# Bias terms rounded sooner, and the integers of the last tiles by another way, in an attention and int8 feed-forward kernel

## What is computed

```python
def layernorm(x): return (x - mean(x)) / sqrt(var(x) + 1e-5)

q      = layernorm(x)                                  # (8, 512, 512)
scores = einsum('bqd,bkd->bqk', q, ctx) / 0.72
attn   = softmax(scores) * mask
x1     = x + (einsum('bqk,bkd->bqd', attn, ctx) + attn_bias) @ W

h       = layernorm(x1)
x_scale = max(amax(abs(h), -1), 1e-6) / 127
x_q     = clip(round(h / x_scale), -128, 127)          # int8
out     = x1 + (x_q @ weight_q.T) * x_scale * weight_scale + ffn_bias
```

## Time and profile before

| | |
|---|---|
| time, median of 3 runs | 327.37 us (326.77 to 328.47) |
| profiled execution, time and span | 327.26 us, 325.1 us |
| TensorE matmul busy | 316.5 us, 97% |
| VectorE busy | 288.8 us, 89% |
| ScalarE, GpSimd busy | 236.0 us, 73%; 222.9 us, 69% |

### The profile page before, as it was taken

How to read it: one execution, slowest core, us unless ns; L and a number is a source line. 1 busy time by engine, 2 the same in 40 slices (tenths; PEclk the granted TensorE clock), 3 DMA queues, 4 the chain that set the end, 5 groups by cost and what they waited for, 6 DMA issues and landing times.

```text
span 325.1 us, 6047 instructions
## 1 busy us (share of the span) xinstructions
PE 316.5 (97%) x1522; PEld 254.8 (78%) x1522; DVE 288.8 (89%) x568; ACT 236.0 (73%) x440; POOL 222.9 (69%) x359
## 2 busy tenths in 40 slices
PE   7999999999999999999999999999999999999993
PEld 7878877778877777887777788877777887777781
DVE  2888889999999999999999999999999999989986
ACT  4466778787778778777777877787787777756651
POOL 3274667677787767678776777877677787766563
PEclk9999999999999999999999999999999999999999
DMA  7997848667485855658595664748667485432002
GB/s 214 272 226 187 196 147 205 190 158 202 146 210 163 219 171 159 196 145 210 161 213 174 161 197 150 203 161 209 178 155 199 144 211 162 126 116 98 33 33 97
DMA packets 69248, 55.26 MB, mean 170 GB/s; under 512 B 21488, under 2 KB 51952, under 8 KB 69232
## 3 DMA queue, kind: packets, MB, share of 16 engines
q1 hardware_dynamic: 61312, 40.65, 49.2%
q10 hardware_dynamic: 7920, 14.42, 13.2%
HBM read 34.87 MB, written 16.25 MB: 157 GB/s over the span
## 4 chain that ended last, share of the span: by engine, by line
PE 90%; DMA 3%; DVE 2%; ACT 1%; SPq 1%; issue 0%; ACTq 0%
PE ps_scores L555 9%; PE ps_scores L557 9%; PE ps_scores L556 9%; PE ps_attn L557 9%; PE ps_attn L555 9%; PE ps_attn L556 9%; PE ps_vw L555 8%; PE ps_vw L557 8%; PE ps_vw L556 8%; PE ps_ffn L716 8%; PE ps_pt L547 4%; DMA x_in<-in_x_dram 2%; DMA ctx_in<-in_ctx_dram 1%; SPq L426 1%; PE ps_pt L543 1%; PE ps_ut L547 1%
## 5 line engine op out<-in xcount | busy, mean ns | idle before, releaser
L1277 POOL TENSOR_TENSOR ct_lo<-ct_raw,ct_hi 128x512 fp32r<-128x512 f32 x28 | 36.2, 1293 | 20.9 <-ACT ct_hi L768 20.9
L555 PE MATMUL ps_vw<-w_hi,ct_hi 128*128 128x512 f32 x116 | 50.5, 435 | 0.0
L555 PE MATMUL ps_attn<-vw_hi,pt_hi 128*128 128x512 f32 x124 | 48.9, 395 | 0.0
L555 PE MATMUL ps_scores<-ct_hi,xt_hi 128*128 128x512 f32 x124 | 48.7, 393 | 0.0
L557 PE MATMUL ps_attn<-vw_hi,pt_lo 128*128 128x512 f32 x124 | 48.4, 391 | 0.0
L557 PE MATMUL ps_scores<-ct_hi,xt_lo 128*128 128x512 f32 x124 | 48.3, 389 | 0.0
L556 PE MATMUL ps_scores<-ct_lo,xt_hi 128*128 128x512 f32 x124 | 48.2, 389 | 0.0
L556 PE MATMUL ps_attn<-vw_lo,pt_hi 128*128 128x512 f32 x124 | 48.2, 389 | 0.0
L1270 POOL TENSOR_TENSOR out_tile<-ffn_out,x_plus 128x512 f32<-128x512 f32 x31 | 40.3, 1299 | 8.6 <-DVE ffn_out L1020 8.6
L557 PE MATMUL ps_vw<-w_hi,ct_lo 128*128 128x512 f32 x116 | 45.4, 391 | 0.0
L556 PE MATMUL ps_vw<-w_lo,ct_hi 128*128 128x512 f32 x116 | 45.3, 390 | 0.0
(11 more groups left out here) (163 smaller groups left out, 776.6 us busy)
## 6 DMA issues: line engine op xcount, KB each, us to landing
x_in<-in_x_dram SPq DMA_DIRECT2D x32, 256.0 KB, 3.1
mask_in<-in_mask_BxSxS_fk_dram SPq DMA_DIRECT2D x32, 256.0 KB, 3.2
norm_rows<-x_norm ACTq DMA_DIRECT2D x30, 256.0 KB, 2.3
x_blocks<-norm_rows SPq DMA_DIRECT2D x120, 64.0 KB, 2.4
ctx_in<-in_ctx_dram SPq DMA_DIRECT2D x56, 128.0 KB, 3.3
out_dram<-out_tile ACTq DMA_DIRECT2D x25, 256.0 KB, 2.5
out_dram<-out_tile SPq DMA_DIRECT2D x6, 256.0 KB, 2.0
ctx_in<-in_ctx_dram SPq DMA_DIRECT2D x4, 256.0 KB, 3.9
```

The lines of the kernel that those rows point to most:

```text
L555: nc.tensor.matmul(bank_, lhs_hi(t), rhs_hi(t), start=(t == 0), stop=False)
L1277: nc.gpsimd.tensor_tensor(ct_lo[:, batch_of(n), :, j * P:(j + 1) * P], ct_raw[:, slot(n, 2), :, :], ct_hi[:, batch_of(n), :, j * P:(j + 1) ...
```

## The change

Four parts. bias_terms is rounded by ScalarE ahead of the first step, and VectorE makes bias_terms_lo ahead of the first two vw_lo. BY_PE goes from 26 to 28, so the integers of tiles 26 and 27 are transposed by DMA, issued by SyncE in the last batch's steps 0 and 1; the product of tile 27 on TensorE and its scaling on VectorE move behind the attention of tile 29 and behind pt_lo of tile 30. The integers of tile 31 are rounded, transposed and copied in two halves, into two banks (ps_ut, ps_pt). The last outputs are made as a product with the weight scales and then a scale-and-add, in place of a product with both scales and then a sum. The diff below goes through SyncE, TensorE (turn_integers, feed_forward, the last steps), ScalarE (ahead of the first step, where the rounding stood behind two split_vw before; clear_integers; the last steps) and VectorE (round_last, finish_last, the first step, the last steps) in this order.

```diff
-BY_PE = TAIL - 2
+BY_PE = TAIL
...
+        last_ut_banks = [ps_ut, ps_pt]
...
-                if exists(base, d - 2) and not last_batch(base):
+                if exists(base, d - 2) and (in_loop(base) or base + d - 2 < BY_PE):
                     wait_count(sp, x1_int_ready, base, d - 2 + 1)
...
                     if is_tile(base, n, LAST):
-                        pe.wait_ge(last_x1_int_ready, 1)
-                    else:
-                        wait_count(pe, x1_int_ready, base, n + 1)
+                        pe.wait_ge(xq_t_ready, base + n - BY_PE)
+                        for h in range(2):
+                            pe.wait_ge(last_x1_int_ready, h + 1)
+                            for t in range(h * NT // 2, (h + 1) * NT // 2):
+                                turned = nc.tensor.transpose(last_ut_banks[h][:, :].bitcast(BF16)[:, t * P:(t + 1) * P],
+                                                             x1_int[:, slot(n, 2), t * P:(t + 1) * P],
+                                                             identity16[:, :])
+                            turned.then_inc(ut_done, 1)
+                        return
+                    wait_count(pe, x1_int_ready, base, n + 1)
...
                             for t in range(NT):
+                                if t == NT // 2:
+                                    pe.wait_ge(xq_t_ready, base + n + 2 - BY_PE)
...
-                    if d > 0 and exists(base, d):
+                    if d > 0 and exists(base, d) and not is_tile(base, d - 2, TAIL):
                         feed_forward(d - 3)
                     if exists(base, d - 1):
                         attend(d - 1)
+                    if is_tile(base, d - 2, TAIL):
+                        feed_forward(d - 3)
                     if exists(base, d + 1):
                         turn_probs(d)
+                    if is_tile(base, d - 2, BY_PE):
                         turn_integers(d - 2)
...
             normalise(HEAD, PER_BATCH + 1)
+            act.wait_ge(bias_terms_ready, NT)
+            nc.scalar.activation(bias_terms_hi[:, :], bias_terms[:, :], ACT.Copy).then_inc(bias_hi_ready, 1)
...
+                    if is_tile(base, n, LAST):
+                        for h in range(2):
+                            act.wait_ge(ut_done, base + n + 1 + h - BY_PE)
+                            nc.scalar.activation(flat(xq_t[:, slot(n, 2), h * NT // 2:(h + 1) * NT // 2, :]),
+                                                 last_ut_banks[h][:, :].bitcast(BF16)[:, half_of(h)],
+                                                 ACT.Copy).then_inc(xq_t_ready, 1)
+                        return
...
-                late = last_batch(base) and exists(base, d + 1)
+                late = is_tile(base, d - 2, BY_PE)
...
+                    for h in range(2):
+                        nc.vector.tensor_scalar(x1_round[:, slot(n, 2), half_of(h)], x1_neg[:, slot(n, 2), half_of(h)],
+                                                col(neg_gain, n), ROUND_MAGIC, ALU.mult,
+                                                ALU.add).then_inc(last_x1_round_ready, 1)
...
+                        nc.vector.tensor_scalar(x1_int[:, slot(n, 2), half_of(h)], x1_round[:, slot(n, 2), half_of(h)],
+                                                ROUND_MAGIC, None, ALU.subtract).then_inc(last_x1_int_ready, 1)
...
-                        nc.vector.scalar_tensor_tensor(out=last_out[:, half_of(h)], in0=last_ffn_banks[h][:, 0:HALF],
-                                                       scalar=col(x_scale, n), in1=wscale_wide[:, half_of(h)],
-                                                       op0=ALU.mult, op1=ALU.mult).then_inc(last_ffn_out_ready, 1)
+                        nc.vector.tensor_tensor(last_out[:, half_of(h)], last_ffn_banks[h][:, 0:HALF],
+                                                wscale_wide[:, half_of(h)], ALU.mult).then_inc(last_ffn_out_ready, 1)
                         dve.wait_ge(last_ffn_out_ready, h + 1)
-                        nc.vector.tensor_tensor(last_out[:, half_of(h)], last_out[:, half_of(h)],
-                                                last_x1_plus[:, half_of(h)], ALU.add).then_inc(last_out_ready, 1)
+                        nc.vector.scalar_tensor_tensor(out=last_out[:, half_of(h)], in0=last_out[:, half_of(h)],
+                                                       scalar=col(x_scale, n), in1=last_x1_plus[:, half_of(h)],
+                                                       op0=ALU.mult, op1=ALU.add).then_inc(last_out_ready, 1)
...
                 if is_tile(base, d, 0):
+                    dve.wait_ge(bias_hi_ready, 1)
+                    lo_part(bias_terms_lo[:, :], bias_terms[:, :], bias_terms_hi[:, :], bias_lo_ready)
                     for t in range(2):
                         split_vw(base, d + t, first_vw_banks[t])
-                    dve.wait_ge(bias_hi_ready, 1)
-                    lo_part(bias_terms_lo[:, :], bias_terms[:, :], bias_terms_hi[:, :], bias_lo_ready)
...
-                if last_batch(base) and d > 0 and exists(base, d):
+                if last_batch(base) and d > 0 and exists(base, d) and not is_tile(base, d - 2, TAIL):
                     scale_ffn(d - 3)
...
                 if exists(base, d) and not is_tile(base, d, LAST):
                     split_probs(d)
+                if is_tile(base, d - 2, TAIL):
+                    scale_ffn(d - 3)
```

More of the change, by code:

```diff
@@ L697, in feed_forward @@
                 def feed_forward(n):
-                    if last_batch(base):
+                    if isinstance(base, int) and base + n >= BY_PE:
                         pe.wait_ge(xq_t_ready, base + n + 1 - BY_PE)
@@ L879, in step @@
                         split_vw(base, d + t, first_vw_banks[t])
-                    act.wait_ge(bias_terms_ready, NT)
-                    nc.scalar.activation(bias_terms_hi[:, :], bias_terms[:, :], ACT.Copy).then_inc(bias_hi_ready, 1)
                     act.wait_ge(first_xt_done, 2)
@@ L1083, in round_last @@
                     dve.wait_ge(neg_gain_ready, TILES)
[L1084 to L1090, removed]
+                    for h in range(2):
+                        nc.vector.tensor_scalar(x1_round[:, slot(n, 2), half_of(h)], x1_neg[:, slot(n, 2), half_of(h)],
+                                                col(neg_gain, n), ROUND_MAGIC, ALU.mult,
+                                                ALU.add).then_inc(last_x1_round_ready, 1)
+                        dve.wait_ge(last_x1_round_ready, h + 1)
+                        dve.wait_ge(ut_done, TILES - 2 - BY_PE)
+                        nc.vector.tensor_scalar(x1_int[:, slot(n, 2), half_of(h)], x1_round[:, slot(n, 2), half_of(h)],
+                                                ROUND_MAGIC, None, ALU.subtract).then_inc(last_x1_int_ready, 1)
                 def finish_last():
```

## The result

The changed kernel took 332.23 us (median of 4 runs, 331.88 to 333.73) against 327.92 for the kernel before on the same chip: a ratio of the means of 1.0141, 95% interval 1.0093 to 1.019. The profiled execution took 332.10 us, its span is 330.3 us against 325.1. The direction was forecast; the size, 330.9 us with a range to 332.3, was not quite: the median is 1.3 us above the forecast, at the very edge of the range, and the mean of the four runs, 332.5, is outside it.

What follows compares the result with a forecast made beforehand. TensorE was taken as the bound, nine tenths of the chain. First step 0.2, stall 3.27 and end 0.2 made 3.66 us on 327.26: 330.9 us, range 329.3 to 332.3.

Steps and rivals of the forecast that it cites:

- the last one issued 1.32 later: SyncE's queue, last steps: the last of tile 31's four loads is issued 1.32 us after the first, 1.75 for four.
- D: Last steps: VectorE's turn of tile 31's rows, and all that follows it, late by 3.06 us; 2.6 to 4.1 by landing.
- a rival at 0.06: TensorE's clock falls to 1.2 GHz in the new gap; scores of tile 31 take 2.84 us more: 333.7 us, chance 0.06.
- the first step: VectorE's early subtraction loses the shared port to GpSimd, so TensorE's bias product starts later: +0.2 us.
- The bound, and SyncE's queue: TensorE bounds; in SyncE's in-order queue, the wait for tile 27's integers holds up output 25's store and tile 31's loads.
- the prediction's other case: First step: VectorE takes the port first and the bias product starts 0.6 us sooner: 330.1 us in all, chance 0.28.
- GpSimd ahead: First step: of two nearly tied starts, 21.17 and 21.24, GpSimd's comes first and holds the shared port.
- GpSimd's queue: Last steps: rstd of tile 29 waits behind the sum of output 27, making VectorE's q_range 0.55 us late.
- The transposes off TensorE: Two groups of four transposes leave TensorE, 0.20 us each: 0.4 us gained, but swallowed by the stall.
- The end: Integers of tile 31 in halves and last sums as scale-and-add: +0.2 us together, bounds 0 and +0.5.
- stall +0.83: Last steps: probs of tile 31 come 3.27 us later, from VectorE's delay of 3.06 plus 0.2 by GpSimd's queue.

Runs made afterwards that it cites:

- the wait alone: Kernel before plus one SyncE wait for the integers of tile 27, ahead of the store of output 25 and tile 31's loads; no DMA transposes: 329.53 us, ratio 1.0087.
- the store later: Changed kernel with the store of output 25 behind the loads of tile 31's rows in SyncE's queue: 331.74 us, ratio 1.0151.
- changed again: The changed kernel as it is, run again on another chip: 332.25 us, ratio 1.0152 to the kernel before.
- integers alone: Kernel before with only the integers of 26 and 27 transposed by DMA and product 27 and its scaling later: 332.83 us, ratio 1.0184.

## Why the prediction was right in direction and wrong in size

The mechanism was right; the sum was short by two of its steps. The term "the last one issued 1.32 later" in D measured 2.93 us, and the lower clock, left out of the sum as a rival at 0.06, cost 1.98 us in the profile. What the first step gave hid 1.17 us of this.

- **The bound, and SyncE's queue: right.** The wait was named, and what stood behind it. Transpose, store and loads came within 0.3 us of the forecast on the shifted clock; the wait alone costs 2.8 us, some 1.2 of it by a late landing.
- **D, the stall of VectorE: undersized, the step that failed.** The term "the last one issued 1.32 later" was 2.93 (296.50 to 299.43), for the issue of 1.94 us that coincides with a packet of q8 instruction; the landing was 2.1 against 2.3. So D was 4.39, not 3.06, and outside its bounds of 2.6 to 4.1. The term came from groups of four loads of 1.74 to 1.90 us; the whole trace of before has none above 2.27. It does have single issues of 1.78 and 1.30 us in the same queue (the rows at 43.60 and 72.72), 1.35 and 0.87 above the usual 0.43. D was bounded by the landing alone, and the issue got no bound.
- **The clock: weighed wrongly, the second step that failed.** It was a rival at 0.06, priced at 2.84 us, and cost 1.98, since the clock was back before the last scores ended. The trace of before has no such gap, so it spoke neither for nor against; I read it as against. The gap was in the forecast, 302 to 304.9 without work and transposes up to 306; measured it is 3.65 us, 301.48 to 305.13. So it should have had a large chance. The Trainium skill ("TensorE: Matmul & The Clock Gate", Why this matters for your kernels) advises against such idle gaps between bursts; the trace agrees, with 0.50 in the window behind the gap.
- **The first step: the wrong side of the tie.** +0.2 forecast, -0.76 here, of which the prediction's other case has 0.6; the rest, or more, can be the execution (see above). Both cases and their mechanism were in the prediction and both appear in the runs. The tie was read off the starts of the kernel before, 0.07 us apart; the step that failed is "GpSimd ahead", a choice that those rows could not carry. The 0.07 was the overlap of VectorE's starts with the ends before them, which the prediction named and did not take off.
- **GpSimd's queue: right as a mechanism, idle in the sum.** In the changed kernel the slow scores cover it: q_range waits for nothing. It costs 0.68 to 0.84 us of VectorE once the scores come in time, where 0.55 was forecast, and moving the product back gained 0.4% between two runs on different chips (1.0001 to 0.9963, whose intervals just overlap).
- **The transposes off TensorE: right**, 0.2 ahead of the stall and 0.25 where nothing swallows them.
- **The end: right in size.** 0.2 forecast, 0.08 in the trace; alone it can't be told from nothing.

Against the forecast of 3.66 the span's 5.19 is made of: first step -1.17 (0.2 forecast, -0.97 with the transposes of 26 counted here), stall +0.83 (4.10 with what the hand-overs gave, against 3.27), clock +1.98, end -0.12. Two errors that added and one that took away left the time 1.3 us off. That the median comes so near the range is in part luck: with the first step as forecast it would have been some 333.4 us.

What stays open: what starts the packet that the slow issue coincides with, and whether the loads would be issued in 1.75 us without it; no run moved it by itself.

## What to carry to other kernels

Before work goes into a queue that issues in order, list what stands behind it and when each landing is needed: here the same transpose costs 5 us ahead of four loads and nothing behind them. Once a forecast contains a gap of some us on TensorE, price the clock as a main case, not as a rival, even if the trace has no such gap to show. A near tie at a shared port is two outcomes, to be carried with two chances; a load that lands half a microsecond late can turn it. And a bound for an issue is taken from the slowest issues of its queue in the whole trace, not from the ones beside the change.

## What the runs showed of the hardware

- Gap in front of TensorE, time of the next scores of tile 31 (2.84 us at full clock), by kernel: 1.48 us, 2.85 (the wait alone); 2.87 us, 5.06 (the store later); 3.57 us, 3.81 (changed again); 3.62 us, 4.20 (integers alone); 3.65 us, 4.82 (changed). Behind the gap of 1.48 us the granted clock stayed at full, behind the four of 2.87 us and more it fell to the lower level; what that cost doesn't grow with the gap.
- In the last steps a plain issue on SyncE's queue takes 0.3 to 0.6 us, mostly 0.43. The 27 of more than 1.1 us (1.13 to 1.94, transposes left out) in 14 profiles all fall on a 16 KB packet of the queue q8 instruction and end 0.2 to 0.4 us behind it. In the last steps that happens only with the transpose of tile 27 ahead of the loads (1.57 to 1.94 us).
- GpSimd's 128x512 subtraction took 1.84 us in place of 1.29 beside a VectorE operation of 0.67 that started at the same moment: the 0.55 more is nearly the whole of VectorE's operation.
